# Attention on one core: one 512-query value product a step, four turn and score pairs in a row, the unit's copy between two exps

## The reference

```python
q, k, v = (proj(wq, bq), proj(wk, bk), proj(wv, bv))   # 16 heads of 8
scores = jnp.einsum('bhqd,bhkd->bhqk', q, k) * (1.0 / math.sqrt(H))
attn = jax.nn.softmax(scores, axis=-1)
out = jnp.einsum('bhqk,bhkd->bhqd', attn, v)
x = _layernorm(x + out.transpose(0, 2, 1, 3).reshape(B, L, D) @ wo.T + bo)
...
h = jax.nn.silu(_tlin(x, w1_w, w1_s)) * _tlin(x, w2_w, w2_s)
h = jax.nn.gelu(_tlin(h, h1_w, h1_s), approximate=False)
h = jax.nn.gelu(_tlin(h, h2_w, h2_s), approximate=False)
x = _layernorm(x + _tlin(h, w3_w, w3_s))
```

## Time and profile before

| | |
|---|---|
| median of 3 runs | 471.4 us |
| the profiled execution's own time | 472.66 us |
| its span | 470.9 us |
| PE busy | 450.0 us, 96% |
| DVE busy | 394.0 us, 84% |
| ACT busy | 365.5 us, 78% |
| POOL busy | 86.7 us, 18% |
| mean granted TensorE clock | 0.992 |

### The profile page before, as it was taken

How to read it: one execution, slowest core, us unless ns; L and a number is a source line. 1 busy time by engine, 2 the same in 40 slices (tenths; PEclk the granted TensorE clock), 3 DMA queues, 4 the chain that set the end, 5 groups by cost and what they waited for, 6 DMA issues and landing times.

```text
span 470.9 us, 9453 instructions
## 1 busy us (share of the span) xinstructions
PE 450.0 (96%) x3630; PEld 213.1 (45%) x3632; DVE 394.0 (84%) x442; ACT 365.5 (78%) x678; POOL 86.7 (18%) x138
## 2 busy tenths in 40 slices
PE   8899999999999999999999999999899799998992
PEld 5333343333333333333343333434343478776882
DVE  6899999999999999999999999999753347647435
ACT  3402898989889899898988989999868786588671
POOL 8400000000000010000000001362511262037002
PEclk9999999999999999999999999999999999999998
DMA  5666430400413050042123004121021000000001
GB/s 157 155 184 201 145 115 3 91 3 2 71 24 114 15 79 3 1 93 60 56 50 43 3 4 91 15 40 53 3 39 47 14 6 1 2 1 22 24 1 45
DMA packets 15547, 24.48 MB, mean 52 GB/s; under 512 B 4560, under 2 KB 8400, under 8 KB 15120
## 3 DMA queue, kind: packets, MB, share of 16 engines
q1 hardware_dynamic: 14864, 23.22, 20.8%
q10 hardware_dynamic: 640, 0.66, 0.8%
HBM read 14.82 MB, written 7.47 MB: 47 GB/s over the span
## 4 chain that ended last, share of the span: by engine, by line
PE 77%; DVE 11%; ACT 5%; issue 2%; POOL 2%; DMA 2%; ACTq 0%; POOLq 0%; DVEq 0%
PE ps L1036 31%; PE ps L1090 29%; PE ps L1174 11%; DVE negmax L798 8%; PE ps L1073 2%; ACT arena L542 2%; DMA qx<-parts_q 1%; ACT hid L582 1%; DVE hf L889 1%; ACT v_pad L576 1%; PE ps L992 1%; PE ps L1123 1%; DVE stats L844 1%; PE ps L1001 1%; ACT hid L592 1%
## 5 line engine op out<-in xcount | busy, mean ns | idle before, releaser
L798 DVE TENSOR_REDUCE negmax<-ps 128x1 f32<-128x1024 f32 x256 | 309.5, 1223 | 6.6 <-PE ps L1036 3.6
L542 ACT ACTIVATE arena<-ps 128x512 f32<-128x512 f32 x512 | 275.1, 597 | 38.9 <-PE ps L1073 15.8
L1036 PE MATMUL ps<-kx,qx 61*128 61x512 f32 x512 | 186.3, 443 | 2.3 <-DMA qx<-parts_q 1.3
L1073 PE MATMUL ps<-qx,kx 64*128 64x512 f32 x512 | 182.2, 450 | 0.0
L1090 PE MATMUL ps<-arena,v_pad 128*32 128x256 f32 x2048 | 163.8, 392 | 1.1 <-ACT arena L542 1.1
L1036 PEld LDWEIGHTS ps<-kx,qx 61*128 61x128 f32 x512 | 75.4, 184 | 101.3 <-DVE negmax L798 85.6
L1090 PEld LDWEIGHTS ps<-arena,v_pad 128*32 128x32 f32 x2048 | 40.5, 108 | 88.1 <-issue 51.3
L1073 PEld LDWEIGHTS ps<-qx,kx 64*128 64x128 f32 x512 | 75.7, 184 | 8.2 <-issue 4.9
L1174 PE MATMUL ps<-hid,w_high 128*128 128x512 f32 (+1 forms) x296 | 67.6, 386 | 1.1 <-ACT hid L592 1.0
L1174 PEld LDWEIGHTS ps<-hid,w_high 128*128 128x128 f32 x296 | 54.3, 188 | 12.6 <-ACT hid L592 1.8
L898 DVE TENSOR_TENSOR hid<-hf,hid 128x512 fp32r<-128x512 f32 x32 | 21.9, 689 | 25.4 <-ACT hid L592 25.4
(11 more groups left out here) (71 smaller groups left out, 226.8 us busy)
## 6 DMA issues: line engine op xcount, KB each, us to landing
kx<-parts_k SPq DMA_DIRECT2D x32, 128.0 KB, 3.7
qx<-parts_q SPq DMA_DIRECT2D x60, 64.0 KB, 3.4
late_sb<-in_late SPq DMA_DIRECT2D x3, 1280.0 KB, 6.6
parts_q<-prt SPq DMA_DIRECT2D x3, 512.0 KB, 4.5
parts_q<-arena SPq DMA_DIRECT2D x3, 512.0 KB, 5.1
xT_sb<-in_xT SPq DMA_DIRECT2D x4, 256.0 KB, 3.7
xT_sb<-arena SPq DMA_DIRECT2D x28, 32.0 KB
prt<-den SPq DMA_DIRECT2D x7, 128.0 KB
```

The source lines that it names most:

```text
L542: nc.scalar.activation(probs[:, n // HG % 2, heads(n), :], ps[:, PLAN["score", n][0], :], ACT.Exp, scale=SCALE).then_inc(exp_done, 1)
L798: nc.vector.tensor_reduce(negmax[:, t // TURNS % 2, h * QT + q:h * QT + q + 1], ps[:, bank:bank + 2, :], AX.XY, ALU.max, negate=True)\
L1036: ins = nc.tensor.matmul(ps[:, MAX_BANK + 2 * (t % 2) + part, :], qx[at, slot, qc, h, q * P:(q + 1) * P], kx[at, slot, h, part * C:(part + ...
L1073: nc.tensor.matmul(ps[:, bank, :], kx[at, slot, h % PAIR, kt * P:(kt + 1) * P], qx[at, slot, qc, h % PAIR, :], start=True, stop=True)\
```

## The change

The work is the same; its grouping and order change.

- The product of a step is made in one piece over all 512 queries: four matmuls of 512 columns in place of two times four of 256.
- On PE a step is now: turn t part 0, score, turn t part 1, score, turn t+1 part 0, score, turn t+1 part 1, score, and then the whole product. Before, half of the product stood between the two turns.
- On ACT the copy of a finished unit moves from the end of its last step to behind the second exp of the step after.
- The bank plan follows: the product of a new unit takes its bank after four scores of the step, not after two. `TURN_AT` puts the transposes at the same places.

```diff
-    for h in range(-2, HALVES_ALL - 2):
-        if h in TURN_AT:
-            place(("max", TURN_AT[h]))
-        for n in (2 * h + HG, 2 * h + HG + 1):
+    for k in range(-1, STEPS_ALL):
+        if k in TURN_AT:
+            place(("max", TURN_AT[k]))
+        for n in range((k + 1) * HG, min((k + 2) * HG, SCORES)):
...
-        if h >= 0 and h % (2 * KT) == 0:
-            w = h // (2 * KT)
+        if k >= 0 and k % KT == 0:
+            w = k // KT
...
+            def copy_unit(w):
+
+                act.wait_ge(pv_done, (w + 1) * KT)
+                nc.scalar.activation(attn_flat[:, w * C:(w + 1) * C], ps[:, PLAN["pv", w][0], :], ACT.Copy)\
+                   .then_inc(unit_out, 1)
...
+                for n in range((k + 1) * HG, min((k + 2) * HG, SCORES)):
+                    exp(n)
+                    if n % HG == 1 and k > 0 and k % KT == 0:
+                        copy_unit(k // KT - 1)
...
-                if h > 0 and h % (2 * KT) == 2 * KT - 1:
-                    act.wait_ge(pv_done, h // 2 + 1)
-                    nc.scalar.activation(attn_flat[:, h // (2 * KT) * C:(h // (2 * KT) + 1) * C],
-                                         ps[:, PLAN["pv", h // (2 * KT)][0], :], ACT.Copy).then_inc(unit_out, 1)
+            copy_unit(U_ALL - 1)
...
-                at = slice(part * HALF, (part + 1) * HALF)
                 for n in range(HG):
-                    ins = nc.tensor.matmul(ps[32 * n:32 * n + 32, PLAN["pv", w][0], at], v_pad[:, w // QC % 2, kt, n, :],
-                                           probs[:, h // 2 % 2, n, at], start=(kt == 0 and part == 0),
-                                           stop=(kt == KT - 1 and part == 1),
+                    ins = nc.tensor.matmul(ps[32 * n:32 * n + 32, PLAN["pv", w][0], :], v_pad[:, w // QC % 2, kt, n, :],
+                                           probs[:, k % 2, n, :], start=(kt == 0), stop=(kt == KT - 1),
                                            tile_position=(0, 32 * n))
...
-                for x in range(2):
-                    if TURNS + LEAD + h < U_ALL * TURNS:
-                        turn(TURNS + LEAD + h, x)
-                    if 2 * h + HG + x < SCORES:
-                        score(2 * h + HG + x)
-                if h >= 0:
-                    product(h)
+                for x in range(HG):
+                    t, n = TURNS + LEAD + 2 * k + x // 2, (k + 1) * HG + x
+                    if t < U_ALL * TURNS:
+                        turn(t, x % 2)
+                    if n < SCORES:
+                        score(n)
+                if k >= 0:
+                    product(k)
```

More of the change, by code:

```diff
@@ L63 @@
 LEAD = 9
-THALF = 10
+TSTEP = 5
 PER = 4
@@ L77 @@
 JOB_BANKS = [0, 1, 6, 7]
-HALF = C // 2
-HALVES_ALL = 2 * U_ALL * KT
+STEPS_ALL = U_ALL * KT
 SCORES = U_ALL * KT * HG
 TAIL = (U_ALL * TURNS - TURNS - LEAD + 1) // 2 + 1
-TURN_AT = {2 * KT * (w - 1) + THALF: w for w in range(1, U_ALL)}
+TURN_AT = {KT * (w - 1) + TSTEP: w for w in range(1, U_ALL)}
 def heads(n):
@@ L550, in copy_max @@
                 nc.scalar.activation(mT[:, w % 2, :], turned(w), ACT.Copy).then_inc(max_copied, 1)
+            def copy_unit(w):
+                act.wait_ge(pv_done, (w + 1) * KT)
+                nc.scalar.activation(attn_flat[:, w * C:(w + 1) * C], ps[:, PLAN["pv", w][0], :], ACT.Copy)\
+                   .then_inc(unit_out, 1)
             copy_max(0)
[L553 to L560, removed]
+            for k in range(-1, STEPS_ALL):
+                if k in TURN_AT:
+                    copy_max(TURN_AT[k])
+                for n in range((k + 1) * HG, min((k + 2) * HG, SCORES)):
+                    exp(n)
+                    if n % HG == 1 and k > 0 and k % KT == 0:
+                        copy_unit(k // KT - 1)
+                if k - STEPS * (ITERS - 1) in W_STEPS:
+                    n = W_STEPS.index(k - STEPS * (ITERS - 1))
                     if n == 0:
@@ L1075, in score, with product @@
                   .then_inc(scores, 1)
[L1077 to L1087, removed]
-                at = slice(part * HALF, (part + 1) * HALF)
+            def product(k):
+                w, kt = k // KT, k % KT
+                if kt == 0 and w % QC == 0:
+                    pe.wait_ge(v_staged, w // QC + 1)
+                pe.wait_ge(exp_done, k * HG + HG)
+                if kt == 0:
+                    bank_free(PLAN["pv", w][1])
                 for n in range(HG):
-                    ins = nc.tensor.matmul(ps[32 * n:32 * n + 32, PLAN["pv", w][0], at], v_pad[:, w // QC % 2, kt, n, :],
-                                           probs[:, h // 2 % 2, n, at], start=(kt == 0 and part == 0),
-                                           stop=(kt == KT - 1 and part == 1),
+                    ins = nc.tensor.matmul(ps[32 * n:32 * n + 32, PLAN["pv", w][0], :], v_pad[:, w // QC % 2, kt, n, :],
+                                           probs[:, k % 2, n, :], start=(kt == 0), stop=(kt == KT - 1),
                                            tile_position=(0, 32 * n))
-                if part == 1:
-                    ins.then_inc(pv_done, 1)
+                ins.then_inc(pv_done, 1)
             pe.wait_ge(v_ready, NC_)
@@ L1148, in _ @@
                       STEPS - 5: (turn_x1, 0), STEPS - 3: (turn_x1, 1)}
-            for h in range(-2, HALVES_ALL):
-                if h in TURN_AT:
-                    turn_max(TURN_AT[h])
-                for x in range(2):
-                    if TURNS + LEAD + h < U_ALL * TURNS:
-                        turn(TURNS + LEAD + h, x)
-                    if 2 * h + HG + x < SCORES:
-                        score(2 * h + HG + x)
-                if h >= 0:
-                    product(h)
-                k = h // 2 - STEPS * (ITERS - 1)
-                if h % 2 == 1 and k in BEHIND:
-                    stage, *of = BEHIND[k]
+            for k in range(-1, STEPS_ALL):
+                if k in TURN_AT:
+                    turn_max(TURN_AT[k])
+                for x in range(HG):
[6 more added lines that the diff above has]
+                    product(k)
+                if k - STEPS * (ITERS - 1) in BEHIND:
+                    stage, *of = BEHIND[k - STEPS * (ITERS - 1)]
                     stage(*of)
```

## The result

The changed kernel takes 487.8 us (median of 4 runs, 487.4 to 488.8) against 471.4 for the kernel before on the same chip: ratio 1.035, 95% interval 1.0335 to 1.0368. It is 16.4 us slower; 14.5 were forecast (485.9, range 473 to 494). The profiled execution took 487.76 us with a span of 486.0.

The account below looks back on a forecast made before the run. The prediction took PE to set the pace before, and the three-bank score ring after. 115 x 0.14 = +16.1, +0.9 and -2.5 gave +14.5 us on 471.4: 485.9, own range 479 to 493, stated range 473 to 494.

Parts of the forecast that it names:

- What bounds the kernel: Steps 0 to 114: PE sets the pace at 2.46 us a step, DVE having about 0.1 us to spare each half step.
- DVE's circle: Turn t+3 waits for the reduce of t+1: 4.83 us over two steps, or 2.41 us a step.
- The ring of score banks: Steady steps: the fourth score waits for the first one's exp, 2.60 us a step against 2.46, 0.14 longer.
- The product by column: Whole product on PE: 0.99 us to the next turn in place of 1.12, each added 256-column stream costing 0.215.
- rival 3: Steady steps: the whole product costs two halves, 1.12 us, so 2.73 a step and 500.9 us; chance 0.05.
- rival 2: Steady steps: the product costs by instruction, not column, 0.78 us, so 2.39 a step and 461.7 us; chance 0.09.
- The load ahead of the product: Between fourth score and product on PE: the 0.11 us weight load isn't hidden, load to load taking 0.43 us.
- rival 1: Steady steps: the load before the product is hidden, 2.49 us a step and 473.3 us; chance 0.10.
- Unit's first product: A new unit's product waits for the second score's exp, 1.67 us into the step against 1.61: 0.06 us a unit.
- The unit's copy and the weight rounding: On ACT: the copy is hidden; with a weight rounding, three of the last 32 steps lose 0.3 us each, 0.9 in all.
- The last steps: Steps without turns, four banks: -1.5 us from 350.67 to 368.88 and -1.0 from 339 to 350, together -2.5.
- rival 4: All steps: new idle time lowers the clock to 1.2 GHz, 1.4 us more a step, 630 us; chance 0.02.

Follow-up runs that it names:

- experiment 1: Changed kernel with both turn parts in one PSUM bank, the reduce reading it twice, and the freed bank joining the scores as a fourth: 465.65 us, ratio 0.988.
- experiment 5: Changed kernel with the first exp of each step up to the last turn doing only 256 of 512 queries: 467.4 us, ratio 0.992.
- experiment 8: Kernel before's half products in steps 0 to 115, changed kernel's order in step -1 and from step 116: 470.7 us, ratio 0.9977 to the kernel before.
- experiment 3: Changed kernel with its order, but the product in two pieces of 256 queries one behind the other: 489.4 us, ratio 1.038.

## Why the prediction was right

- **What bounds the kernel.** PE by its stream, with DVE close behind. Right: with one bank more and a shorter PE stream, the step went to 2.42, DVE's circle, and no further (experiments 1 and 5).
- **The ring of score banks.** The decisive step, and the runs show it from three sides: a fourth bank removes the loss, a shorter first exp removes it and a shorter second doesn't, and the fourth score's load stands 0.05 us behind the first exp's end in the trace. The circle was 0.53 + 0.60 + 0.05 + 0.43 + 0.99 = 2.60, and it is 0.54 + 0.60 + 0.05 + 0.42 + 1.00 = 2.61 (202.01, 202.55, 203.15, 203.20, 203.62, 204.62). In 115 steps this is 17.6 us at 0.153 a step, where I had 16.1. Most of the 1.5 us is rounding: 2.60 was a sum of numbers read to 0.01. The size of the step, the place of the wait and the term that decides are therefore all as forecast.
- **The product by column.** 1.00 us from its load to the next step, 0.99 forecast; twice a half (rival 3) and one stream more (rival 2) are out.
- **The load ahead of the product.** Not hidden: 0.42 us from the lone score's load to the product's, so rival 1 is out.
- **Unit's first product.** 0.06 forecast, 0.15 measured. In the step at 173 us the second exp ends at 173.34 + 1.08 = 174.42 and the product starts at 174.57, 0.15 behind it, where a score's load stands 0.05 behind the exp it waits for:

```profile
173.34 1.08 ACT L541 ACTIVATE arena<-ps 128x512 f32<-128x512 f32 x2 [0.56 <-PE ps L1076]
...
174.54 0.19 PEld L1091 LDWEIGHTS ps<-arena,v_pad 128*32 128x32 f32 x8 [0.37 <-issue]
174.57 1.06 PE L1091 MATMUL ps<-arena,v_pad 128*32 128x512 f32 x8
```

  The 0.09 us beyond the forecast make 1.3 us in 14 units. What makes this wait longer is not settled; the product has two waits in a row there, for the exps and for the bank.
- **The unit's copy and the weight rounding.** Hidden but for three steps, as forecast, but these cost less. Steps 97, 105 and 113 take 2.80 us in place of 2.61, 0.6 in all where I had 0.9; and the kernel before already had one such step, which I overlooked (105, 2.75 us in place of 2.46), so the change pays 0.3. It fits what 17.6 and 1.3 leave of the stretch of 19.3 us, 0.4.
- **The last steps.** The term with a wrong reason. I forecast -2.5 by the order; the trace gave -3.0, which looks close, but that is luck: experiment 8 splits what lies behind the transpose into 1.2 for the order and 1.6 for a clock that didn't fall in that execution. I had the low clock of the kernel before in the earlier trace rows, used it for a rival only, and took those steps to cost the same after.
- **The clock in the steady steps** (rival 4) stayed at 1.00, with a gap of some 0.4 us in each step.
- **The sum.** The traces differ by 15.1 us where 14.5 were forecast, nearer than the terms are. These missed by +1.5 (the ring), +1.3 (a unit's first product), -0.5 (copy and rounding), -0.5 (the last steps) and -1.1 (the prologue, where I had nothing), and the misses largely cancel. The mechanism is right; that the sum is good to 0.6 us is luck.

## What to carry to other kernels

Before issuing the consumers of a buffer ring closer together, add up the ring's own circle: from a fill to its reader's end and back to the fill that takes the same buffer. With three banks no four scores may stand closer than fill, exp and signal (1.19 us here), so a product that the order spreads between them is free, and one pushed out behind them is paid in full. An engine that reads 95% busy can still be waiting; compare instructions and starts, not shares. A part of a reordering can be right where its conditions hold: here the whole-step order is a gain of 1.2 us in the last steps, which have no turns and a fourth bank (which of the two it needs was not separated).

## What the runs showed of the hardware

- The latency, not the throughput, of a single ACT instruction set the pace: four exps in a row take 2.07 us of a step of 2.61, and halving one of them took 20 us off the kernel, halving its neighbour 1.3.
- Two float32 half products in a row cost as much as a whole one within 0.006 us a step, with eight weight loads more (experiment 3): these loads are hidden.
- After 1.5 to 1.7 us without matmuls, the granted clock fell in six of ten traced executions (to 0.65 and 0.50, and to 0.57 and 0.58, over 4 us in two of them) and not in the other four, among them the changed kernel's. A fall cost 1.5 to 1.6 us where the same kernel was traced with and without it. Ten filler matmuls in that pause left it at 1.00 in both kernels that were given them, and were worth 1.1 to 1.2 us of the whole kernel.
